# Gated cross-attention and mixture of experts: value sums in fp32, decay operands joined into one product a group

## The reference

```python
log_D = log_fg_mat + ig[:, None, :]                 # cs[s] - cs[t] + ig[t], masked
D_mat = exp(log_D - max_log_D)
C = (qk / sqrt(DH)) * D_mat
normalizer = maximum(abs(C.sum(-1)), exp(-max_log_D))
h = einsum('hst,htd->hsd', C / (normalizer + EPS), vh)
```

## Time and profile before

| | us |
|---|---|
| median of 3 runs | 853.86 (852.61 to 853.98) |
| profiled execution, own time | 853.17 |
| its span from first to last instruction | 851.4 |
| TensorE busy (products) | 723.2 |
| VectorE busy | 601.0 |
| GpSimd busy | 411.7 |
| ScalarE busy | 336.1 |
| mean granted TensorE clock | 0.781 of full |

### The profile page before, as it was taken

How to read it: one execution, slowest core, us unless ns; L and a number is a source line. 1 busy time by engine, 2 the same in 40 slices (tenths; PEclk the granted TensorE clock), 3 DMA queues, 4 the chain that set the end, 5 groups by cost and what they waited for, 6 DMA issues and landing times.

```text
span 851.4 us, 18263 instructions
## 1 busy us (share of the span) xinstructions
PE 723.2 (85%) x6260; PEld 574.7 (68%) x6260; DVE 601.0 (71%) x1523; ACT 336.1 (39%) x874; POOL 411.7 (48%) x366
## 2 busy tenths in 40 slices
PE   5938988898978989602589999999999999999994
PEld 3514655566555656502479899898888988899893
DVE  8455999999999999789355555565565555555552
ACT  3333535335344344204334434444344344343441
POOL 0062777777767867400223534445443444534433
PEclk9975555555555555555699999999999999999998
DMA  9635666766667573214338969879798887978862
GB/s 289 225 133 148 217 202 223 225 200 230 202 199 248 185 220 129 69 13 179 138 128 241 316 209 286 261 230 314 229 281 248 250 284 237 274 245 249 265 172 51
DMA packets 85483, 179.72 MB, mean 211 GB/s; under 512 B 14738, under 2 KB 48019, under 8 KB 85395
## 3 DMA queue, kind: packets, MB, share of 16 engines
q1 hardware_dynamic: 62866, 140.10, 50.2%
q0 software_dynamic: 13824, 18.43, 10.1%
q10 hardware_dynamic: 8704, 20.06, 6.3%
HBM read 140.93 MB, written 38.67 MB: 211 GB/s over the span
## 4 chain that ended last, share of the span: by engine, by line
PE 53%; DVE 33%; issue 9%; DMA 2%; ACT 1%; DVEq 1%; POOL 1%; SPq 0%; POOLq 0%
PE bank L1024 44%; DVE Cl L562 10%; DVE Cm L554 3%; DVE y L650 2%; PE bank L288 2%; PE bank L1018 2%; PE bank L291 2%; DVE st L630 1%; DVE n L595 1%; DVE st L621 1%; DVE x L641 1%; DVE R L919 1%; PE bank L301 1%; DVE n L597 1%; DMA out<-res,TS 1%
## 5 line engine op out<-in xcount | busy, mean ns | idle before, releaser
L1024 PE MATMUL bank<-xh,w 128*128 128x256 bf16 (+1 forms) x1760 | 269.4, 263 | 9.8 <-DVE xl L1080 8.2
L1024 PE MATMUL bank<-xl,w 128*128 128x256 bf16 (+1 forms) x880 | 223.1, 263 | 0.0
L1006 POOL DMA_INDIRECT out<-res,TS x72 | 115.7, 1608 | 215.1 <-DVE res L1141 135.7
L1024 PEld LDWEIGHTS bank<-xh,w 128*128 128x128 bf16 x1760 | 166.1, 98 | 29.1 <-issue 12.2
L1097 ACT ACTIVATE sg<-bank 128x256 f32<-128x256 f32 (+1 forms) x240 | 86.8, 362 | 231.8 <-PE bank L1024 226.6
L1127 DVE TENSOR_TENSOR hf<-sg,bank 128x256 f32<-128x256 f32 (+1 forms) x200 | 78.9, 394 | 122.4 <-ACT sg L1097 118.4
L1024 PE MATMUL bank<-w,hh 128*128 128x256 bf16 x864 | 140.0, 273 | 0.0
L562 DVE TENSOR_TENSOR Cl<-Cm,Ch 128x512 bf16<-128x512 f32 x64 | 117.0, 1866 | 0.4 <-issue 0.3
L446 POOL TENSOR_TENSOR whl<-wst,whl 128x1224 bf16<-128x1224 f32 x32 | 92.1, 2879 | 47.7 <-ACT whl L434 47.7
L997 POOL DMA_INDIRECT xg<-y_d,TG x72 | 72.3, 1004 | 85.4 <-DVE TS L954 53.0
L1024 PE MATMUL bank<-w,hlo 128*128 128x256 bf16 x360 | 98.1, 273 | 0.0
(11 more groups left out here) (213 smaller groups left out, 1167.1 us busy)
## 6 DMA issues: line engine op xcount, KB each, us to landing
w<-w_d SPq DMA_DIRECT2D x40, 1408.0 KB
w<-w_d SPq DMA_DIRECT2D x40, 768.0 KB
wst<-in_wts SPq DMA_DIRECT2D x32, 612.0 KB, 4.2
w_d<-whl ACTq DMA_DIRECT2D x32, 612.0 KB, 4.9
vb<-in_kv SPq DMA_DIRECT2D x8, 528.0 KB, 6.2
xa<-in_x SPq DMA_DIRECT2D x8, 512.0 KB, 8.3
kT<-in_kv SPq DMA_DIRECT2D x8, 512.0 KB, 8.8
xc<-in_x SPq DMA_DIRECT2D x8, 512.0 KB, 5.7
```

The lines of the kernel that those rows point to most:

```text
L1006: nc.gpsimd.indirect_dma_start(out, bass.IndirectOffsetOnAxis(ap=TS[:, c0:c0 + 1], axis=0), res[w][:, j, :], None, bounds_check=TOK - 1, o ...
L1024: mm = nc.tensor.matmul(dst, l, r, start=(n == 0), stop=(n == len(pairs) - 1))
```

## The change

The value sums take `Cm` and v as they are, in fp32, one product a head. `Ch`, `Cl` and the split of v are gone, and with them `b_ch_act`, `b_cl_dve` and `b_v_pool`. In the log decay of a group, one product of 512 columns over 24 rows takes the place of five: `asb` holds 12 rows of `ga` parts (3 parts by 4 heads) above 12 rows of ones, `mx` holds 12 rows of a 0/1 selection above 12 rows that carry the parts of `-gm` in the columns of their head. The ones, the zeros and the selection are written once, at the start (memsets on GpSimd, a copy of 4096 elements a partition on ScalarE for each of the two buffers); the rest comes per batch in five DMAs instead of one. Some tiles change their place in SBUF (`late`).

```diff
-        am_d = dram("am_d", [NB, 3 * NH, 2, S], BF16)
+        a_d = dram("a_d", [2 * NB, 3, HG, S], BF16); m_d = dram("m_d", [2 * NB, HG, 3, S], BF16)
...
-        vb = [attn(f"vb{w}", [P, NC, NH * DV]) for w in range(2)]
-        EB = [attn(f"EB{w}", [P, 2, S]) for w in range(2)]; qE = [attn(f"qE{w}", [P, D]) for w in range(2)]
-        amb = [attn(f"amb{w}", [24, 2, S], BF16) for w in range(2)]
-        Dm = [[attn(f"Dm{w}{g}", [P, 512]) for g in range(2)] for w in range(2)]
-        Cm = [[attn(f"Cm{w}{g}", [P, 512]) for g in range(2)] for w in range(2)]
-        Ch = [attn(f"Ch{k}", [P, 512], BF16) for k in range(4)]
-        Cl = [attn(f"Cl{k}", [P, 512], BF16) for k in range(4)]
-        vp = [attn(f"vp{w}", [P, 2, NH, DV], BF16) for w in range(2)]
+        vb = [attn(f"vb{w}", [P, NC, NH * DV]) for w in range(2)]; qE = [attn(f"qE{w}", [P, D]) for w in range(2)]
+        asb = [attn(f"asb{w}", [24, 2, S], BF16) for w in range(2)]; mx = [attn(f"mx{w}", [24, 2, HG, S], BF16) for w in range(2)]
...
             nc.gpsimd.memset(wwin[:, :, :], 0.0).then_inc(s_wz, 1)
+            for w in range(2):
+                nc.gpsimd.memset(mx[w][:, :, :, :], 0.0).then_inc(s_mz, 1)
+                nc.gpsimd.memset(asb[w][:, :, :], 1.0).then_inc(s_mz, 1)
...
+        def mx_act(act, w):
+            act.wait_ge(s_mz, 2 * w + 1)
+            nc.scalar.copy(mx[w][0:12, :, :, :], sel12[:, :].unsqueeze(1).unsqueeze(3).to_broadcast([12, 2, HG, S])).then_inc(s_sel, 1)
...
                 w_hi_act(act, n + 2)
+            mx_act(act, 1)
             act.wait_ge(g_dve, 14)
...
         def g_sync(sp):
             for k in range(3):
                 sp.wait_ge(g_pl, (1, 3, 4)[k])
-                sp.dma_start(am_d[:, k * NH:(k + 1) * NH, 0, :], ap[k][:, :]).then_inc(g_am, 16)
+                sp.dma_start(a_d[:, k, :, :], ap[k][:, :]).then_inc(g_am, 16)
                 sp.wait_ge(g_dve, (5, 8, 10)[k])
-                sp.dma_start(am_d[:, k * NH:(k + 1) * NH, 1, :], mp[k][:, :]).then_inc(g_am, 16)
+                sp.dma_start(m_d[:, :, k, :], mp[k][:, :]).then_inc(g_am, 16)
...
+        def b_am_sync(sp, b):
+            w = b % 2
+            sp.dma_start(asb[w][0:12, :, :], a_d[2 * b:2 * b + 2].rearrange("g k j s -> (k j) g s")).then_inc(b_am[w], 16)
+            for j in range(HG):
+                sp.dma_start(mx[w][12 + 3 * j:15 + 3 * j, :, j, :], m_d[2 * b:2 * b + 2, j].rearrange("g k s -> k g s")).then_inc(b_am[w], 16)
+
         def b_sync(sp, b):
             w = b % 2
             ge(sp, b_dl, 2 * NC * (b - 1))
-            sp.dma_start(amb[w][:, :, :], am_d[b:b + 1, :, :, :].rearrange("o k x s -> (o k) x s")).then_inc(b_am[w], 16)
+            b_am_sync(sp, b)
...
         def b_dl_pe(pe, t):
             b, c = t // NC, t % NC
-            am = amb[b % 2][:, :, c * P:(c + 1) * P]
-            ge(pe, b_am[b % 2], b // 2 * 16 + 16)
+            w = b % 2
+            ge(pe, b_am[w], (b // 2 + 1) * 16 * (1 + HG))
             for g in range(2):
                 ge(pe, b_D, 2 * t + g - 1)
                 dl = bank[:, g, :]
                 nc.tensor.matmul(dl, identb[:, :], maskb[:, :].unsqueeze(1).to_broadcast([P, HG, P]),
                                  start=True, stop=False)
-                nc.tensor.matmul(dl, am[:, 0, :],
-                                 sel24[:, g * HG:(g + 1) * HG].unsqueeze(2).to_broadcast([24, HG, P]),
-                                 start=False, stop=False)
-                for j in range(HG):
-                    mm = nc.tensor.matmul(bank[:, g, j * P:(j + 1) * P],
-                                          sel24[:, g * HG + j:g * HG + j + 1].to_broadcast([24, P]), am[:, 1, :],
-                                          start=False, stop=(j == HG - 1))
-                mm.then_inc(b_dl, 1)
+                nc.tensor.matmul(dl, asb[w][:, g, c * P:(c + 1) * P], mx[w][:, g, :, c * P:(c + 1) * P],
+                                 start=False, stop=True).then_inc(b_dl, 1)
 
         def b_pv_pe(pe, t):
             b, c = t // NC, t % NC
...
                     nc.tensor.matmul(hp[:, g, :, :].rearrange("p h e -> p (h e)"), qE[t % 2][:, g * P:(g + 1) * P],
                                      St[(c - 1) % 2][:, g, :], start=(g == 0), stop=False)
             ge(pe, b_kv[b % 2], b // 2 * 16 + 16)
-            ge(pe, b_vl, t + 1)
             for g in range(2):
-                ge(pe, b_Ch, 2 * t + g + 1)
-                k = 2 * (t % 2) + g
+                ge(pe, b_C, 2 * t + g + 1)
                 for j in range(HG):
-                    o = hp[:, g, j, :]
                     hd = g * HG + j
-                    nc.tensor.matmul(o, Ch[k][:, j * P:(j + 1) * P], vp[t % 2][:, 0, hd, :], start=(c == 0 and hd == 0), stop=False)
-                    nc.tensor.matmul(o, Ch[k][:, j * P:(j + 1) * P], vp[t % 2][:, 1, hd, :], start=False, stop=False)
-                ge(pe, b_Cl, 2 * t + g + 1)
-                for j in range(HG):
-                    mm = nc.tensor.matmul(hp[:, g, j, :], Cl[k][:, j * P:(j + 1) * P], vp[t % 2][:, 0, g * HG + j, :],
-                                          start=False, stop=(g == 1 and j == HG - 1))
+                    mm = nc.tensor.matmul(hp[:, g, j, :], Cm[t % 2][g][:, j * P:(j + 1) * P], vv(t)[:, hd * DV:(hd + 1) * DV],
+                                          start=(c == 0 and hd == 0), stop=(hd == NH - 1))
             mm.then_inc(b_h, 1)
...
-        def b_ch_act(act, t):
-            ge(act, b_h, t - 1)
-            for g in range(2):
-                ge(act, b_C, 2 * t + g + 1)
-                nc.scalar.copy(Ch[2 * (t % 2) + g][:, :], Cm[t % 2][g][:, :]).then_inc(b_Ch, 1)
-
-        def b_v_pool(pool, t):
-            b = t // NC
-            ge(pool, b_kv[b % 2], b // 2 * 16 + 16)
-            ge(pool, b_h, t - 1)
-            v3 = vv(t).rearrange("p (h e) -> p h e", e=DV)
-            nc.gpsimd.tensor_copy(vp[t % 2][:, 0, :, :], v3).then_inc(b_vh, 1)
-            ge(pool, b_vh, t + 1)
-            nc.gpsimd.tensor_tensor(vp[t % 2][:, 1, :, :], v3, vp[t % 2][:, 0, :, :], ALU.subtract).then_inc(b_vl, 1)
...
-                ge(dve, b_Ch, 2 * t + g - 3)
-                ge(dve, b_Cl, 2 * t + g - 3)
+                ge(dve, b_h, t - 1)
                 by4 = lambda a: a.rearrange("p (j s) -> p j s", j=HG)
                 nc.vector.scalar_tensor_tensor(by4(Cm[t % 2][g][:, :]), bank[:, 4:8, g * P:(g + 1) * P], SCALE,
                                                by4(Dm[t % 2][g][:, :]), ALU.mult, ALU.mult).then_inc(b_C, 1)
-
-        def b_cl_dve(dve, t):
-            ge(dve, b_h, t - 1)
-            for g in range(2):
-                k = 2 * (t % 2) + g
-                ge(dve, b_Ch, 2 * t + g + 1)
-                nc.vector.tensor_tensor(Cl[k][:, :], Cm[t % 2][g][:, :], Ch[k][:, :], ALU.subtract).then_inc(b_Cl, 1)
...
-            if 0 <= t + 2 < NT:
-                b_ch_act(act, t + 2)
...
-                b_cl_dve(dve, t + 2)
...
-            if 1 <= t + 1 < NT:
-                b_v_pool(pool, t + 1)
...
-            sp.dma_start(amb[0][:, :, :], am_d[0:1, :, :, :].rearrange("o k x s -> (o k) x s")).then_inc(b_am[0], 16)
+            sp.wait_ge(s_mz, 4)
+            b_am_sync(sp, 0)
...
             nc.scalar.preload_act_table_set("natural_log_exp_and_others")
+            mx_act(act, 0)
             a_norm_act(act, 0)
```

More of the change, by code:

```diff
@@ L84, in build @@
         upperb = sb("upperb", [P, P], BF16); onesb = sb("onesb", [P, P], BF16)
-        maskb = sb("maskb", [P, P], BF16); sel24 = sb("sel24", [24, NH], BF16)
-        selt = sb("selt", [24, NH]); blkm = sb("blkm", [P, HG * DV]); blkt = sb("blkt", [P, HG * DV])
+        maskb = sb("maskb", [P, P], BF16); sel12 = sb("sel12", [12, HG])
+        selt = sb("selt", [12, HG]); blkm = sb("blkm", [P, HG * DV]); blkt = sb("blkt", [P, HG * DV])
         eps_c = sb("eps_c", [P, 1]); one_c = sb("one_c", [P, 1])
@@ L98, in build @@
         xc = [sb(f"xc{w}", [P, NC, D]) for w in range(2)]; st2 = sb("st2", [P, NC, 6]); st3 = sb("st3", [P, NC, 6])
-        mv = sb("mv", [P, NC, 2, 2]); lv = sb("lv", [P, NC, 2]); rs = sb("rs", [P, NC, 2])
+        mv = sb("mv", [P, NC, 2, 2]); lv = sb("lv", [P, NC, 2]); rs = sb("rs", [P, NC, 2]); nb = sb("nb", [P, NC, 2])
         x2 = sb("x2", [P, NC, D]); y = sb("y", [P, NC, D])
@@ L122, in build, with late @@
         whl = [attn(f"whl{w}", [P, 2, WCH], BF16) for w in range(2)]
+        late_ctx = ExitStack()
+        def late(name, shape, dt=F32):
+            return late_ctx.enter_context(nc.sbuf_tensor(name, shape, dt))
+        Dm = [[late(f"Dm{w}{g}", [P, 512]) for g in range(2)] for w in range(2)]
+        Cm = [[late(f"Cm{w}{g}", [P, 512]) for g in range(2)] for w in range(2)]
+        EB = [late(f"EB{w}", [P, 2, S]) for w in range(2)]
+        ap = [late(f"ap{k}", [BH, S], BF16) for k in range(3)]
+        mp = [late(f"mp{k}", [BH, S], BF16) for k in range(3)]
+        gE = late("gE", [BH, S]); gd = late("gd", [BH, NC]); gdx = late("gdx", [BH, NC])
+        late_ctx.close()
```

(15 more changed lines are left out.)

5 lines of the change are left out of this document (1 added, 4 removed).

## The result

The changed kernel took 875.54 us (median of 4 runs, 871.64 to 875.83) against 853.38 for the kernel before (median of 4, 852.61 to 853.98): the ratio is 1.025 (95% interval 1.0219 to 1.028). That is slower, inside the range, and 5.0 us under the 880.5 forecast. Its profiled execution took 875.83 us and has a span of 873.8, against 851.4 before, so there are 22.4 us of span to account for.

The account below looks back on a forecast made before the run. VectorE was taken to pace the settled attention slots, TensorE 8% behind and next to bind. 853.2 + 22.0 (slots) + 2.8 (last value sums) + 3.6 (start) - 1.6 (head) = 880.0, stated as 880.5 us; range 862 to 902.

Parts of the forecast that it names:

- The bound changes hands: Settled attention slots: VectorE falls from 35.36 to 19.1 us per four slots, and TensorE runs without gaps as the bound.
- The slot: Attention stage: four slots take 39.1 us against 36.26; the 31 slots take 292.1 against 270.1, +22.0 us.
- Value sums: TensorE, each slot: sixteen fp32 records at 0.226 us, 3.61 us in place of 0.82, 2.79 more.
- The decay: TensorE, each slot: one product for five per group, about 2.1 us in place of 3.03, 0.93 less.
- The last value sums: End of the attention stage: the last tile's value sums end later, +2.8 us.
- The start: Kernel start: ScalarE's 4096-element copy ahead of its first normalisation delays the first transposes, +3.6 us (ends 0 and 7).
- The head: Before the first value sums: five SP transfers +1.2, three tiles' cheaper decays -2.8, together -1.6 us.
- The copy in the gates' gap: `mx_act(1)` on ScalarE falls where it waits for VectorE's gate arithmetic: costs nothing; uncovered 3.6 us.
- Rival 1: Attention stage: gapless TensorE is granted its upper clock level, so DMA and GpSimd bind; 781 us, chance 0.10.
- Rival 2: Value sums: fp32 products cost only their columns, 1.09 us for the eight heads; 799 us, chance 0.03.
- Rival 3: Attention stage: clock up for a fifth of the stretch, 29 us vanish, change about nil (851); chance 0.06.

Follow-up runs that it names:

- decay_only: Kernel before with the joined decay product alone, its bf16 value sums, `Ch` and `Cl` kept: 858.28 us, ratio 1.0069.
- half_values: Changed kernel without the value products of heads 1, 3, 5 and 7, so outputs are not the reference's: 820.7 us in its only run.
- memsets_late: Changed kernel with GpSimd's memsets of `mx` and `asb` issued only after VectorE's constants are done: 870.38 us, ratio 1.0205.

## Why the prediction was right, and where its steps were off

**The bound changes hands: right.** VectorE's 16.3 us of `Cl` in four slots went (35.36 to 20.00; I said 19.1), TensorE took over with no gap, and it was longer than VectorE had been. decay_only shows that VectorE was the bound and half_values that TensorE is.

**The slot: right in kind, over-sized.** 38.00 us for four slots against 39.1 said; 31 slots +14.0 against +22.0. Value sums: 3.39 a slot against 3.61, because a record takes 0.212 and not 0.226; the proportion between 9 and 132 columns over-charged 33 columns, and the row at 9 (0.2175) was itself the better price. That is 7 us over 31 slots. The state's product took 0.88 in its new surroundings where I kept 1.04. The decay, 2.17 against 2.1, was under-charged by 2; logits 0.87 and transposes 0.46 were as said. 38.00 is what these pieces sum to: 4 x (3.39 + 1.17 + 2.17 + 0.87 + 0.46) + 3 x 0.88 + 3 x 1.04 = 38.0.

**The last value sums: right**, +2.55 (3.27 against 0.72) where I said +2.8.

**The start: the step that failed.** I said +3.6, with 7 as the end of the range, and it was +7.2. The copy's 3.6 us on ScalarE were right to the hundredth. Wrong was the clause that a hold-up of VectorE by the memsets wouldn't matter, "since it waits for ScalarE". VectorE makes the constants, and ScalarE's and TensorE's first work waits for the last one, which came at 11.24 instead of 4.05 us. Of these 7.2 us ScalarE's first activation shows 3.8 (11.27 against 7.43), since it had waited for a transfer before; memsets_late moved the transposes forward by 4.1 us with nothing but that changed. The Trainium skill ("SBUF — State Buffer", section "Who interferes with whom") states that VectorE, in a mode that uses two ports, which `tensor_scalar` can enter, contends with GpSimd for a shared pair of ports, and that the one of the two that comes second is blocked for the whole of the other's instruction. The trace agrees as to the blocking: 3.61 us under a memset of 3.64, 0.28 without; which mode the instruction was in, no run here shows. I hadn't weighed it.

**The head: +1.2 didn't come.** SP's five issues took 0.35 + 1.22 us, not five times 0.5, and the first decay came at 76.96 with no idle before it that a DMA ended. The copy in the gates' gap was indeed free: ScalarE waits 3.56 us more behind it. What I said for this stretch, -1.6, was -2.6.

**The range.** The ends were added up to 864 to 905 and the range given was 862 to 902; 875.54 lies in either.

**The rivals.** Rival 1, the clock, fell for this change: 0.50 over 284 us of covered time. The Trainium skill ("TensorE: Matmul & The Clock Gate", section "Why this matters for your kernels") would have it that continuous work brings the full clock; this trace doesn't agree (0.50 throughout), and the trace decides. But its other half, that with a raised clock the change wins by much, held: 807.24 us with 128 rows, against 781 said; the level held for part of the time (mean 0.74), and TensorE waited 22.3 us for q. Rival 2 fell: 0.212 us a record, not 0.068. Rival 3, the upper level for a fifth of the stretch, fell too (0.50 throughout).

The total was 5.0 us too high. That it wasn't further off is in part luck, since the misses cancel: an over-sized slot (8.0) and a delay at the head that didn't come (1.0) stood against an under-sized start (3.6) and 1.2 behind the attention; the rest is in the last value sums (0.3) and in the step from span to median (0.5).

## What to carry to other kernels

Work that is taken off the bounding engine is worth only the distance to the next one, and if it is paid for on that next one it is worth less than nothing: in four slots of 36.26 us TensorE's dense work of 31.7 left 4.6 to give, and the change asked for 10.3 in value sums less 3.4 of decay. Price an fp32 product with a 128x128 weight tile by its records: at the lower level one took 0.2175 us at 9 columns, 0.212 at 33 and 0.26 at 132. And look at what a memset of GpSimd runs beside: at the start of this program each of two long ones added its length to VectorE's constants, which two other engines wait for.
